# Moving the diagonal products and the skip sum within a step of a Mamba-2 block, and leaving out the last chunk's states

## The reference, cut to what matters

```python
H, P, N, G, K, CHUNK = (64, 64, 128, 1, 4, 32)
proj = hidden_states @ in_proj_w                   # gate, x, B, C, dt
hbc = silu(conv4(hbc) + conv_b)                    # x, B, C
scores = einsum('bcihn,bcjhn->bcijh', C_c, B_c) * decay * dt_c
Y_diag = einsum('bcijh,bcjhp->bcihp', scores, x_c)
states = einsum('bclh,bclhn,bclhp->bchpn', decay_states * dt_c, B_c, x_c)
def step(prev, inp):
    st, cd = inp
    new = cd[:, :, None, None] * prev + st
    return (new, prev)                             # chunk c uses the state before it
Y_off = einsum('bclhn,bchpn,bclh->bclhp', C_c, prev_states, exp(cum))
yh = (Y_diag + Y_off) + D_param[None, None, :, None] * x
hidden = yr * silu(gate)                           # then RMS norm, out_proj
```

## Time and profile before

| what | value |
|---|---|
| median of 3 runs | 1360.67 us (1360.49 to 1361.19) |
| the profiled execution | 1359.91 us |
| its span, first to last instruction | 1358.2 us |
| mean granted clock of PE | 0.995 |
| busy share of the span | PE 96%, DVE 87%, ACT 74%, POOL 63% |

### The profile page before, as it was taken

The page is one execution under the profiler, slowest core; times in us unless marked ns, Lnnn a source line. Parts: engine busy times, 40 slices in busy tenths (PEclk is TensorE's granted clock), DMA queues, the critical chain, the costliest instruction groups (busy, mean ns, idle before and its releaser), DMA issues.

```text
span 1358.2 us, 26981 instructions
## 1 busy us (share of the span) xinstructions
PE 1299.9 (96%) x8896; PEld 1111.2 (82%) x8896; DVE 1187.0 (87%) x2651; ACT 1001.7 (74%) x2043; POOL 851.0 (63%) x920
## 2 busy tenths in 40 slices
PE   7999998899999999999999999999999999987998
PEld 7988886678888888888888888888888888876887
DVE  6965567899999999999999999999999999997542
ACT  1135566898888888889888888888898888883432
POOL 1033220268697878778787978787787879674232
PEclk9999999999999999999999999999999999998999
DMA  7110002265555543544555555436446544345000
GB/s 163 80 69 32 17 16 70 71 137 125 108 126 116 119 119 109 115 106 110 120 124 107 123 118 123 112 110 113 106 115 120 123 115 115 100 103 202 16 17 32
DMA packets 98106, 136.51 MB, mean 101 GB/s; under 512 B 23760, under 2 KB 45872, under 8 KB 97840
## 3 DMA queue, kind: packets, MB, share of 16 engines
q1 hardware_dynamic: 97968, 134.78, 41.7%
HBM read 124.78 MB, written 9.96 MB: 99 GB/s over the span
## 4 chain that ended last, share of the span: by engine, by line
PE 56%; DVE 29%; issue 11%; ACT 3%; DMA 0%; DVEq 0%; POOL 0%; SPq 0%; ACTq 0%; POOLq 0%
PE psum L38 13%; PE psum L40 12%; PE psum L39 12%; DVE xs L1266 6%; PE psum L1715 6%; DVE inner L1317 4%; PE psum L1704 4%; PE psum L1495 4%; DVE M L1293 3%; PE psum L1692 3%; DVE xend L1283 3%; DVE psum L1325 3%; DVE mixed L1347 2%; PE psum L1681 1%; DVE carry L1317 1%
## 5 line engine op out<-in xcount | busy, mean ns | idle before, releaser
L826 ACT ACTIVATE M<-cum_row,cum_table 128x128 f32<-128x128 f32 x1024 | 312.1, 390 | 0.0
L1266 DVE SCALAR_TENSOR_TENSOR xs<-psum,conv_w_sb,xs 128x509 f32<-128x509 f32 (+2 forms) x384 | 283.1, 737 | 0.4
L986 POOL TENSOR_TENSOR hid_lo<-hid,hid_hi 128x512 fp32r<-128x512 f32 x128 | 204.9, 1601 | 56.1 <-PE psum L40 49.9
L1032 POOL TENSOR_TENSOR hid<-hid,sg 128x512 f32<-128x512 f32 x128 | 165.8, 1295 | 76.4 <-DVE hid L1334 76.2
L1018 POOL TENSOR_TENSOR squares<-squares,sq 128x512 f32<-128x512 f32 x124 | 161.1, 1299 | 71.8 <-ACT sq L803 71.8
L1293 DVE TENSOR_TENSOR M<-M,CB 128x1024 f32<-128x1024 f32 x128 | 184.4, 1440 | 0.0
L1715 PE MATMUL psum<-M,xdt 128*64 128x128 f32 x2048 | 140.1, 278 | 20.2 <-DVE psum L1325 20.0
L1715 PEld LDWEIGHTS psum<-M,xdt 128*64 128x64 f32 x2048 | 110.1, 136 | 42.8 <-DVE M L1293 24.2
L1692 PE MATMUL psum<-xend,B_tok 128*128 128x128 f32 x1024 | 137.6, 277 | 5.3 <-DVE carry L1317 4.5
L840 ACT ACTIVATE xs<-psum,conv_b_sb,conv_w_sb 128x512 f32<-128x512 f32 x128 | 99.2, 775 | 57.3 <-PE psum L40 56.6
L834 ACT ACTIVATE M<-M 128x1024 f32<-128x1024 f32 x128 | 134.5, 1051 | 0.5
(11 more groups left out here) (197 smaller groups left out, 3379.1 us busy)
## 6 DMA issues: line engine op xcount, KB each, us to landing
cum_row<-cum_scratch SPq DMA_DIRECT2D x256, 256.0 KB, 4.6
e_row<-e_scratch SPq DMA_DIRECT2D x256, 128.0 KB, 3.5
xw_raw<-L_attn_in_proj_w_dram SPq DMA_DIRECT2D x32, 128.0 KB, 5.0
wo_raw<-L_attn_out_proj_w_dram SPq DMA_DIRECT2D x32, 128.0 KB, 4.5
gw_raw<-L_attn_in_proj_w_dram SPq DMA_DIRECT2D x16, 256.0 KB, 5.5
x_res<-_attn_hidden_states_dram SPq DMA_DIRECT2D x4, 512.0 KB, 7.1
x_scratch<-x_res SPq DMA_DIRECT2D x4, 512.0 KB, 2.6
x_res<-x_scratch SPq DMA_DIRECT2D x1, 2048.0 KB, 8.5
```

The source lines that it names most:

```text
L826: last = nc.scalar.activation(M[:, v % 3, h, c * CH:(c + 1) * CH], cum_row[:, v % 2, h, c * CH:(c + 1) * CH], ACT.Relu, bias=scalar_of(CUM ...
L986: nc.gpsimd.tensor_tensor(hid_lo[:], hid[:, v % 2, :], hid_hi[:, v % 2, :].bitcast(F32), ALU.subtract).then_inc(hid_lo_done, 1)
L1032: nc.gpsimd.tensor_tensor(hid[:, v % 2, :], hid[:, v % 2, :], sg[:, v % 8, :], ALU.mult).then_inc(hid_done, 1)
L1266: nc.vector.scalar_tensor_tensor(xs[:, v % 7, shift:], psum[:, X_BANK + v % 2, 0:TT - shift], tap_of(v, step), xs[:, v % 7, shift:], ALU.m ...
```

## The change

Three things are done.

1. On PE, `proj_g(s+8)` moves ahead of `diag(s+1)`. `proj_x(s+8)` stays where it was, and so `cum_sums(1)`, `totals(1)` and `turn_cum(1)` come to stand behind a gate projection.
2. On DVE, `skip_path(s+1)` moves behind tap 2 of the convolution and scan 2.
3. In the last tile `states` makes three products instead of four, and `to_chunk_end` writes three chunks instead of four.

```diff
             def to_chunk_end(v):
...
-                nc.vector.tensor_tensor(xend[:], psum[:, XT_BANK, :].rearrange("p (c h q) -> p c h q", h=2, q=HP),
-                                        per_chunk_head(TO_END, v), ALU.mult).then_inc(xend_done, 1)
+                n = min(CPT, NC - 1 - at_slot(v)[1] * CPT)
+                nc.vector.tensor_tensor(xend[:, 0:n], psum[:, XT_BANK, 0:n * P].rearrange("p (c h q) -> p c h q", h=2, q=HP),
+                                        per_chunk_head(TO_END, v)[:, 0:n], ALU.mult).then_inc(xend_done, 1)
...
                 if alive(s + 2):
                     scan(s + 2, 1)
-                if alive(s + 1):
-                    skip_path(s + 1)
                 if alive(s + 7):
                     conv_tap(s + 7, 2)
                 if alive(s + 2):
                     scan(s + 2, 2)
+                if alive(s + 1):
+                    skip_path(s + 1)
                 if alive(s + 3):
                     times_dt(s + 3)
                     to_chunk_end(s + 3)
...
             def states(v):
...
-                for c in range(CPT):
+                for c in range(min(CPT, NC - 1 - t * CPT)):
...
                 if alive(s + 3):
                     turn_x(s + 3)
+                if alive(s + 8):
+                    proj_g(s + 8)
                 if alive(s + 1):
                     diag(s + 1)
...
                 if alive(s + 8):
-                    proj_g(s + 8)
                     proj_x(s + 8)
```

## The result

The changed kernel takes 1341.95 us (median of 4 runs, 1340.99 to 1344.38) against 1360.58 for the kernel before on the same chips. The ratio is 0.9866, with a 95% interval of 0.9848 to 0.9883. It is faster, by 18.6 us. I had forecast 6.7 us. The time lies inside the whole range (1337 to 1362), but outside the forecast's own (1351 to 1359), and nearest to the first rival (1339), in which M wins the ties.

What follows compares the result with a forecast made beforehand. PE and DVE bound it in turn, then DVE: 117.7 plus M's waits 1.8 and 3.4 is 122.9, plus 0.2 is 123.1 against 124.1 a group; 1359.9 - 7.3 + 1 = 1353.6, median 1354, range 1351 to 1359.

Steps and rivals of the forecast that it cites:

- first rival: M wins the ties with POOL's `hid_hi`, eight waits of 0.42 vanish: 121 us a group, 1339 us; chance 0.25.
- What bounds the kernel: Middle loop: PE and DVE pass the bound to and fro; after the change DVE bounds at 122.9, PE 120.0 a group.
- Entry into half-width products: PE, `diag` behind the gate projection instead of transposes: entry about 0.08 us as in the old order, difference 0.
- slower rival: PE's entry to `diag` behind a 512-column product costs more; at 0.35 us a step, 1372 us; chance 0.08.
- M at 2.24 and `hid_hi` at 2.18: Starts after the skip sum's start, in us: DVE's M at 2.24, POOL's `hid_hi` at 2.18, 0.06 ahead.
- Who wins at 0.06: Ordinary steps: POOL's `hid_hi`, 0.06 us ahead, beats M, which waits 0.42 in eight steps, 3.4 a group.
- The other steps' waits: M's waits in the first and last tile stay at today's mean: 8 x 0.23 = 1.8 us a group.
- second rival: POOL wins everywhere, first and last tile too: new waits 6 us, DVE 124.0 a group, 1360 to 1361; chance 0.24.
- The last chunk: Last tile: fewer `states` products save PE 0.9 us a group, narrower `to_chunk_end` saves DVE 0.5.
- The start: Before s = 0: `turn_cum(1)` behind the gate projection may delay ACT's rows; +1 us, ends 0 and +1.5.
- The tail: Last seven steps, without projections: taken as 0 us, with -2.5 as the other end.

Runs made afterwards that it cites:

- moves_only: The changed kernel with the last chunk's states computed as before, so only the PE and DVE moves: 1346.61 us, ratio 0.9912 to the kernel before.

## Why the prediction was wrong in size

DVE is the next bound, as it said, but the step that sized DVE's new waits failed. By its own steps:

- **What bounds the kernel.** Right. DVE was taken for the next bound and is; PE's lateness moved from the diagonal products to `states`, as written. The margin was too wide: the sum had PE at 120.0 and DVE at 122.9, and in the trace PE is busy for 120.81 and DVE for 121.56.
- **Entry into half-width products.** Right: 0.09 behind a 512-column product as behind transposes, and no extra cost. The slower rival fell with this row.
- **M at 2.24 and `hid_hi` at 2.18.** Right (2.24, and 2.16 to 2.18).
- **Who wins at 0.06.** This is the step that failed. The forecast took "0.06 is nearer to the first" of two examples and charged 8 x 0.42 = 3.4 us a group. M wins at 0.06, in every steady step of the changed kernel, and even at 0.08. The example that led me astray, POOL winning at 0.07, comes from the last seven turns, in which no projections and no convolution run. There POOL wins at 0.06 too. The timelines of POOL and DVE of the kernel with both moves but all states:

```profile
1193.22 0.61 POOL L983 CAST hid_hi<-hid 128x512 fp32r<-128x512 f32 x1
...
1193.28 1.63 DVE L1293 TENSOR_TENSOR M<-M,CB 128x1024 f32<-128x1024 f32 x1
```

  Two rows from different stages, and of different POOL operations, had been read as two points of one scale. Why the line is elsewhere in the last steps is open; it wasn't tried.
- **The other steps' waits.** Also off, the other way. I left today's mean in eight steps, 1.8 us a group. In fact 12 of 16 steps wait, for POOL's gate, 4.3 us in all. I had counted eight ordinary steps in which the gate follows the skip sum at once; there are four, since in the others the squares wait for ACT or follow other work. Against the forecast, M's waits are 3.4 lower here and 2.5 higher there, and DVE's work is 0.4 lower (117.3 instead of 117.7): together the 1.3 us a group by which 123.1 was too high. The two errors in M's waits thus cancel in good part, which is luck.
- **The first rival.** It came nearest, 1339, because it has M winning the ties, and partly by luck. It took PE's 120.0 plus 1 for the bound, where DVE with 4.3 us of waits is, and its 121 a group was 0.8 short. Its sign, a mean of M near 1.3, did not come: the mean is 1.465, and the forecast had 1.54.
- **The second rival.** Its sum is too small: 0.4 to 0.6 in eight steps and the 3.4 of the others are 6.6 to 8.2 us, not 6. By its own condition it would have been slower than before.
- **The last chunk.** 0.5 us of DVE a group was forecast, and 0.43 is what it gives (122.27 against 121.84). How much of that is PE's 0.9 isn't shown, since DVE's idle time falls by 0.4 with it.
- **The start.** +1 was forecast. Step 0 to step 4 takes 1.3 us more, and 0.9 of it goes with the gate projection of turn 0.
- **The tail.** 0 was taken; the part behind step 120 gives 1.1.
- **ACT's wait for the skip sum** was missing. It costs nothing here.

M winning the ties had been given 0.25, but a difference of 0.01 us between two single rows carried the 15 us between 1354 and 1339. A tie like that should have been given as a coin toss: in steps 8 to 119 of the kernel before, no POOL operation starts between 0.03 and 0.17 us ahead of M, so no row of that stage could decide it.

## What to carry to other kernels

When an operation that two engines both want is moved, work out where it lands against the other engine's operations to a tenth of a microsecond. A move that looks free costs or gives whole per cents: +1.6% for the PE order alone, -0.9% with the skip sum moved too (moves_only). Price a reordering as a set, since a part can be harmful alone and the best of the set together. And take the examples for a rule from the stage in which it will be applied; where that stage has none, the rule is a guess.

## What the runs showed of the hardware

- M (both inputs in SBUF) and a POOL operation on SBUF hold each other back whole: M takes up to 2.18 us instead of 1.21 where it comes behind POOL's gate or squares, and the cast takes 1.76 instead of 0.61 where it comes behind M. The Trainium skill, page SBUF — State Buffer, section Who interferes with whom, says the same, and that issue order decides who blocks. By the starts in the traces that holds only from about 0.1 us: POOL's cast wins from 0.10 ahead (M 1.56 at 0.12) and loses up to 0.08 ahead (213 of 215 times; M 1.21, the cast 1.76). In the last steps it wins already at 0.06 and 0.07 (three cases), and why isn't known.
- A wait ends about 0.13 us before the end of the record of the one that was first, in both orders: behind a gate with 0.70 us left M waits 0.57, and the cast that loses to M ends 1.68 behind M's start (665.31 + 1.76 against 665.39), so its own 0.61 begin at 1.07, 0.14 before the end of M's 1.21.
- Entering half-width products costs PE 0.08 to 0.09 us in both cases seen (behind four transposes and behind a 512-column product). Leaving them costs 0.10 in the 6 products behind them (1.50 instead of 1.40).
- In the changed kernel where POOL's gate follows the squares at once it starts 1.24 to 1.26 us behind their start, without a wait between them, and `hid_hi`, which waits for the gate's semaphore, starts about 1.35 behind the gate, though squares and gate take the same 1.28.
- 116 operations of 0.07 us cost 7 us more behind the skip sum than ahead of it.
